# Gated cross-attention on one core: attention weights transposed in pieces of 103 rows that run across heads, whole-tile vector passes, and ScalarE exponentials of one group of heads by head

## Chip, cores and metric

One NeuronCore of a Trainium2 chip runs the whole program in one launch. The metric is the device time in microseconds, taken as the median of several executions; lower is better.

## What is computed

The reference is a decoder of four layers over `x` of 32 x 128 tokens with 128 features. Each layer adds a cross-attention step, gated by `tanh(g_xattn)`, and a feed-forward step, gated by `tanh(g_ffn)`. The change concerns the attention of layers 1, 2 and 3 (called l1x, l2x and l3x below). Cut to what matters, each of them is:

```
q = norm(x) @ Wq          # (32, 128, 128), 16 heads of 8 features
k, v = ctx @ Wk, ctx @ Wv # (32, 77, 128)
a = softmax(q_h @ k_h.T / sqrt(8))   # per head h: 128 queries x 77 keys
x = x + tanh(g_xattn[layer]) * (concat_h(a @ v_h) @ Wo + bo)
```

Layers 1 and 3 have an output bias `bo`, layer 2 has none; layer 1 has a bias on v; layer 3 adds a mask to the scores.

## The kernel before, in words

`attention` (L458) is called three times, for l1x, l2x and l3x; queries (`xnT`), keys (`kT`) and values (`vall`, 77 keys on the partitions) are already in SBUF then. It loops over 32 tiles n, one batch entry of 128 queries each. The 16 heads are four groups g of four heads i. Every engine has its program written out by hand with semaphores between them, and runs it strictly in order:

- GpSimd (`pool`): `keys(n)` (L510) spreads the keys of a tile over a 128 x 308 block, so that one group of heads becomes one matmul. `values(n)` (L517) copies the values of a tile into `Vpad`, zeroed once in `constants` (L127), with a 32-column strip per head. `divide(n)` (L522) multiplies 128 x 1232 exponentials by the reciprocal sums. `add(n)` (L533) adds the gated output to `x`; with an output bias `bias(n)` (L526) adds the gated bias too. In one step of its loop: keys(it+5), values(it+1), add(it-1), bias(it), divide(it+2).
- TensorE (`pe`): `score(n)` (L566) makes four products of 128 x 308 in PSUM banks 2 to 5 (in l3x after four mask products, L562). `turn(n, r)` (L576) transposes the weights of head r of each of the four groups (four transposes of 77 columns, into bank 6 or 7 by turns), for r = 0 to 3. `weigh(n, r)` (L586) multiplies them by the values, four narrow products side by side, summed over r. `output(n)` (L595) applies Wo. The order within a tile is turn 0, turn 1, output(n-1), weigh 0, turn 2, weigh 1, turn 3, weigh 2, score(n+4), weigh 3.
- VectorE (`v`): `shift(n)` takes the largest score of each head (L659) and subtracts it (L664) into `prob`, both in two halves of 8 heads; `total(n)` sums the exponentials in two halves (L672) and takes the reciprocal (L674); `spread` and `joined` (L680, L684) take the statistics of x for the next norm.
- ScalarE (`sc`): `keep_turned(n)` copies each transposed round out of PSUM (L634), with `keep_out(n-1)` (L625) after the second; then `exponent(n+3)` in two halves (L619), then `keep_heads(n)` (L641, L643).

TensorE's score(n+4) waits until the shift of tile n+3 has read the score banks (L559). All tiles use the same four banks, so scores are made for one tile at a time.

Of the kernel before, what the change touches and what calls it, by code (L numbers as in the profile page):

```python
# [21 lines left out]
P = 128  # L22
D = 128
# [54 lines left out]
def constants(nc, t, d):  # L78

    with ExitStack() as ctx:  # L80
# [15 lines left out]
        def _(pool):  # L96
# [29 lines left out]
            for b in range(2):  # L126
                step(pool.memset(t["Vpad"][b][:], 0.0))  # L127
# [330 lines left out]
def attention(nc, t, d, layer, gate_at, bias_v=False, bias_out=False, masked=False):  # L458
# [4 lines left out]

    AHEAD = 4
    GK = HG * KEYS
    with ExitStack() as ctx:
        s = Sems(nc, ctx, layer)
        loads, gb_ready, biased = s.one("loads"), s.one("gb_ready"), s.one("biased")
# [22 lines left out]
        def scores(i):  # L491
            return ps[:, 2 + 2 * i:4 + 2 * i, 0:GK].rearrange("p b (h k) -> p b h k", k=KEYS)

        def heads(a, i):
            return a[:, 8 * i:8 * i + 8].rearrange("p (b h) -> p b h", b=2)

        def probs(n, i):
            return prob[n % 4][:, 8 * i:8 * i + 8, :].rearrange("p (b h) k -> p b h k", b=2)

        @block.sync  # L500
        def _(sp):
            if bias_out:
                sp.dma_start(bo[:], d[f"{layer}_bo"].partition_broadcast(P)).then_inc(loads, 16)

        @block.gpsimd
        def _(pool):
# [30 lines left out]
            if bias_out:  # L537
                pool.wait_ge(loads, 16)
                pool.tensor_scalar(gb[:], bo[:], t["gate"][:, gate_at:gate_at + 1], None, ALU.mult).then_inc(gb_ready, 1)
                pool.wait_ge(gb_ready, 1)  # L540
            for it in range(1 - AHEAD, NT):
# [6 lines left out]
                if bias_out and it >= 0:  # L548
                    bias(it)
# [5 lines left out]
        def _(pe):  # L555
            def score(n):
                pe.wait_ge(kblk_ready, n + 1)
                if n >= 1:
                    pe.wait_ge(shifted, 2 * n)  # L559
# [19 lines left out]
            def weigh(n, r):  # L579
                if r == 0:  # L580
# [3 lines left out]
                pe.wait_ge(turned_kept, 4 * n + r + 1)  # L584
# [3 lines left out]
                if r == HG - 1:  # L588
                    ins.then_inc(heads_made, 1)

            def output(n):
# [23 lines left out]
        def _(sc):  # L615
            def exponent(n):
                for i in range(2):
                    sc.wait_ge(shifted, 2 * n + 1 + i)
                    sc.activation(prob[n % 4][:, 8 * i:8 * i + 8, :], prob[n % 4][:, 8 * i:8 * i + 8, :], ACT.Exp, scale=scale).then_inc(exped, 1)  # L619
# [25 lines left out]
            for n in range(AHEAD - 1):  # L645
                exponent(n)
# [2175 lines left out]
```

## Time and profile before

| | us |
|---|---|
| median of 3 runs | 1613.0 |
| range of the runs | 1606.56 to 1613.46 |
| the profiled execution | 1609.98 |
| its span in the trace | 1608.2 |
| l1x, start of the first and of the last transpose | 236.3 and 389.8 |
| l2x, the same | 770.1 and 922.9 |
| l3x, the same | 1053.8 and 1224.5 |

Over the span TensorE is busy 77%, VectorE 62%, GpSimd 55% and ScalarE 51%. These shares mix a dozen stages; the three attention stages take about 520 us of the span together, and only they are changed but for one memset. In a timeline row the first number is the start and the second the time from the start of the first of its instructions to the end of the last; the distance between the starts of successive rows of one engine is what an operation really costs that engine, since instructions overlap a little.

### The profile page before, as it was taken

The page shows a single profiled execution, that of the slowest core. Times are in us where ns is not written, and L with a number is a line of the kernel's source. Part 1 is how long each engine was busy: PE and PEld are TensorE (multiplying, and loading weights), DVE is VectorE, ACT ScalarE, POOL GpSimd, SP SyncE. Part 2 cuts the span into 40 slices and gives each one's busy share as a digit, 9 for nine tenths or more (in the row PEclk, how much of TensorE's full clock was granted, in tenths as well). Part 3 has the DMA queues.
Part 4 walks back from the last instruction along what each step waited for, and adds up shares of the span by engine and source line. Part 5 has one row for each costly group of instructions (what it writes and reads, how often), then busy time and mean ns, then how long its engine had stood idle before and what let it go on. Part 6 is the DMA issues. An engine that isn't in the chain of part 4 may idle for free. (4 is left out here: it accounts for less than half of the span.)

```text
span 1608.2 us, 27318 instructions
## 1 busy us (share of the span) xinstructions
PE 1233.3 (77%) x9890; PEld 857.0 (53%) x9890; DVE 1004.2 (62%) x2128; ACT 821.8 (51%) x1584; POOL 888.1 (55%) x1106
## 2 busy tenths in 40 slices
PE   4773569997459996444899968689997774989994
PEld 4432546664359994333566535455656553565553
DVE  5789869995531111344999769688882687443421
ACT  2487448886635453144788766467775431212120
POOL 5200148885245554651677578367775345478775
PEclk9796779999679998667899979889997795999997
DMA  2000000000238883110000000000000004344442
GB/s 102 7 0 0 1 2 2 2 2 5 59 111 240 238 230 85 40 31 9 2 1 2 2 16 1 2 2 1 2 2 1 24 33 146 76 80 97 94 88 23
DMA packets 51798, 74.98 MB, mean 47 GB/s; under 512 B 8169, under 2 KB 31602, under 8 KB 51282
## 3 DMA queue, kind: packets, MB, share of 16 engines
q1 hardware_dynamic: 35858, 55.01, 10.7%
q0 software_dynamic: 15808, 18.24, 6.8%
q8 instruction: 80, 1.31, 0.3%
q14 instruction: 52, 0.43, 0.1%
HBM read 57.09 MB, written 16.12 MB: 46 GB/s over the span
## 5 line engine op out<-in xcount | busy, mean ns | idle before, releaser
L1616 PE MATMUL ps<-topk_up_sb,topk_wu 128*128 128x512 f32 x256 | 124.1, 632 | 2.9 <-DVE sb_xnT L1736 2.2
L1517 ACT ACTIVATE topk_ga<-ps 128x512 f32<-128x512 f32 x64 | 38.3, 599 | 155.5 <-PE ps L1616 152.7
L1440 POOL DMA_INDIRECT out<-topk_shared,l3f_route_slots x64 | 100.2, 1566 | 18.1 <-issue 18.0
L1736 DVE TENSOR_TENSOR sb_xnT<-topk_ga,ps 128x512 f32<-128x512 f32 x64 | 43.9, 688 | 103.3 <-ACT topk_ga L1517 99.7
L207 POOL TENSOR_SCALAR sb_stage<-sb_x,l0f_rstd,l0f_shift 128x128 f32<-128x128 f32 x48 | 24.6, 525 | 146.3 <-DVE l0f_shift L194 146.1
L2095 DVE TENSOR_TENSOR l1f_g_y<-ps,l1f_g_wd 128x256 f32<-128x256 f32 x39 | 16.6, 425 | 136.1 <-PE ps L2038 100.2
L2065 ACT ACTIVATE l1f_g_h<-ps,l1f_g_wd 128x256 f32<-128x256 f32 x156 | 63.3, 475 | 73.6 <-DMA l1f_g_wd<-l1f_W 49.9
L522 POOL TENSOR_TENSOR l3x_prob<-l3x_prob,l3x_rden 128x1232 f32<-128x1232 f32 x32 | 72.0, 2249 | 51.1 <-DVE l3x_rden L674 51.1
L522 POOL TENSOR_TENSOR l2x_prob<-l2x_prob,l2x_rden 128x1232 f32<-128x1232 f32 x32 | 72.0, 2249 | 44.4 <-DVE l2x_rden L674 44.4
L634 ACT ACTIVATE l3x_pt<-ps 77x512 f32<-77x512 f32 x128 | 72.7, 592 | 39.7 <-PE ps L576 39.7
L522 POOL TENSOR_TENSOR l1x_prob<-l1x_prob,l1x_rden 128x1232 f32<-128x1232 f32 x32 | 72.0, 2249 | 32.5 <-DVE l1x_rden L674 32.5
L634 ACT ACTIVATE l2x_pt<-ps 77x512 f32<-77x512 f32 x128 | 72.6, 592 | 32.5 <-PE ps L576 29.1
L634 ACT ACTIVATE l1x_pt<-ps 77x512 f32<-77x512 f32 x128 | 72.7, 592 | 30.4 <-PE ps L576 29.5
L1436 POOL DMA_INDIRECT topk_xg<-l3f_rows,l3f_route_slots x64 | 76.7, 1198 | 18.9 <-issue 18.3
L1977 POOL DMA_INDIRECT l1f_g_xg<-l1f_rows,l1f_route_slots x78 | 75.2, 964 | 17.7 <-issue 12.7
L1616 PEld LDWEIGHTS ps<-topk_up_sb,topk_wu 128*128 128x128 f32 x256 | 49.7, 204 | 55.6 <-issue 50.0
L576 PE MATMUL ps<-sb_ident,l1x_prob 128*77 128x128 f32 x512 | 78.9, 288 | 0.0
L576 PE MATMUL ps<-sb_ident,l2x_prob 128*77 128x128 f32 x512 | 78.6, 287 | 0.0
L576 PE MATMUL ps<-sb_ident,l3x_prob 128*77 128x128 f32 x512 | 78.4, 286 | 0.0
L2029 PE MATMUL ps<-l1f_g_xgT,l1f_g_wu 128*128 128x256 f32 x312 | 76.0, 388 | 2.2 <-issue 2.1
L2038 PE MATMUL ps<-l1f_g_wd,l1f_g_h 128*128 128x128 f32 x624 | 75.9, 275 | 0.0
L2038 PEld LDWEIGHTS ps<-l1f_g_wd,l1f_g_h 128*128 128x128 f32 x624 | 72.7, 192 | 0.1
(500 smaller groups left out, 3588.5 us busy)
## 6 DMA issues: line engine op xcount, KB each, us to landing
l1f_g_wd<-l1f_W SPq DMA_DIRECT2D x39, 322.0 KB
l1f_g_wu<-l1f_W SPq DMA_DIRECT2D x39, 256.0 KB
topk_wu<-l3f_W SPq DMA_DIRECT2D x16, 512.0 KB
l1f_y_rows<-l1f_g_y SPq DMA_DIRECT2D x39, 128.0 KB
topk_wd<-l3f_W SPq DMA_DIRECT2D x16, 256.0 KB
l3f_rows<-l3f_route_own_rows SPq DMA_DIRECT2D x1, 2304.0 KB, 8.0
sb_x<-x SPq DMA_DIRECT2D x1, 2048.0 KB
l1f_rows<-l1f_route_own_rows SPq DMA_DIRECT2D x1, 2048.0 KB
```

Of the source, the lines that this page charges most:

```text
L522: pool.tensor_tensor(prob[n % 4][:], prob[n % 4][:], rden[n % 2][:].unsqueeze(2).broadcast_to([P, HEADS, KEYS]), ALU.mult).then_inc(normed, 1)
L576: ins = pe.transpose(ps[0:KEYS, 6 + r % 2, g * P:g * P + P], prob[n % 4][:, HG * g + r, :], t["ident"][:])
L634: sc.activation(pt[n % 2][:, r, :, :].rearrange("k h q -> k (h q)"), ps[0:KEYS, 6 + r % 2, :], ACT.Copy).then_inc(turned_kept, 1)
L1436: pool.indirect_dma_start(out=xg[g % R][:, i, :], out_offset=None, in_=u["rows"], in_offset=spot(g, i)).then_inc(row_came[g % R], 16)
L1440: pool.indirect_dma_start(out=out_rows, out_offset=spot(g, i), in_=y[g % 2][:, i, :], in_offset=None, compute_op=ALU.add).then_inc(y_added ...
L1517: sc.activation(gx[c % 2][:], ps[:, 2 * (c % 2), :], ACT.Gelu).then_inc(x_acted, 1)
L1616: ins = pe.matmul(ps[:, 2 * (c % 2) + i, :], wu[g % W][:, (i * CX + c) * P:(i * CX + c + 1) * P], xgT[g % 2][:], start=True, stop=True)
L1736: v.tensor_tensor(xh[g % 2][:, c, :], gx[c % 2][:], ps[:, 2 * (c % 2) + 1, :], ALU.mult).then_inc(x_ready, 1)
L1977: pool.indirect_dma_start(out=xg[r][:, i, :], out_offset=None, in_=u["rows"], in_offset=bass.IndirectOffsetOnAxis(ap=u["slots"][:, g * G + ...
L2029: pe.matmul(ps[:, c, 0:GS], wu[g % W][:, c * P:(c + 1) * P], xgT[g % 2][:], start=True, stop=True).then_inc(made, 1)
L2038: ins = pe.matmul(ps[:, 4 + g % 2, i * P:(i + 1) * P], h[g % 2][:, c, i * P:(i + 1) * P], wd[g % W][:, c * P:(c + 1) * P], start=(c == 0), ...
L2065: sc.activation(h[g % 2][:, c, :], ps[:, c, 0:GS], ACT.Gelu, bias=wd[g % W][:, C * P + c:C * P + c + 1]).then_inc(acted, 1)
```

## The change

Transposing goes by 103 consecutive columns of a group's 308 instead of by head: three rounds per tile (103, 103 and 102 columns) instead of four. The rows of the transposed weights then belong to more than one head, so the values have to be laid out in the same order: SyncE brings them with seven DMAs per four tiles from `vall` into `vrows`, and GpSimd multiplies them by a mask that is 1 where row and column belong to the same head. `Vpad` and its memsets go. The output bias becomes a product of one row on TensorE. VectorE takes the largest of all 16 heads in one instruction, subtracts and sums 12 heads in one instruction each; the last group's four heads are done by ScalarE alone, by head, straight from PSUM, with bias `-scale * max` (`negate`, VectorE) and the sum in the accumulator. score(n+4) now waits for this step (`direct`) too.

The core of the diff:

```diff
-            for b in range(2):
-                step(pool.memset(t["Vpad"][b][:], 0.0))
...
+    PIECES, L = 3, 103
+    FROM = [(0, 0, 0, 77), (0, 77, 0, 26), (1, 0, 26, 51), (1, 51, 0, 52), (2, 0, 52, 25), (2, 25, 0, 77), (2, 102, 0, 1)]
+    MV = 4
+    DG = GROUPS - 1
+    DH = HG * DG
...
         def _(sp):
             if bias_out:
-                sp.dma_start(bo[:], d[f"{layer}_bo"].partition_broadcast(P)).then_inc(loads, 16)
+                sp.dma_start(bo[:], d[f"{layer}_bo"].partition_broadcast(1)).then_inc(loads, 16)
+            for j in range(NT // MV):
+                if j >= 2:
+                    sp.wait_ge(vpad_ready, MV * (j - 1))
+                for c, row, key, n in FROM:
+                    sp.dma_start(vrows[j % 2][row:row + n, c, :], t["vall"][key:key + n, j * MV * P:(j + 1) * MV * P]).then_inc(v_here[j % 2], 16)
...
-                pool.tensor_copy(bass.AP(tensor=vpad[n % 2], offset=0, ap=[[HEADS * 32, KEYS], [HG * 32, GROUPS], [32 + HD, HG], [1, HD]]),
-                                 t["vall"][:, n * P:(n + 1) * P].rearrange("k (g i c) -> k g i c", g=GROUPS, i=HG)).then_inc(vpad_ready, 1)
+                j = n // MV
+                if n % MV == 0:
+                    pool.wait_ge(v_here[j % 2], 16 * len(FROM) * (j // 2 + 1))
+                pool.tensor_tensor(vpad[n % 2][:], vrows[j % 2][:, :, (n % MV) * P:(n % MV + 1) * P], vmask[:], ALU.mult).then_inc(vpad_ready, 1)
...
-            def bias(n):
-                xb = t["x"][:, n * P:(n + 1) * P]
-                pool.tensor_tensor(xb, xb, gb[:], ALU.add).then_inc(biased, 1)
...
+            step = Chain(pool, mask_step)
+            step(pool.memset(own_head[:], 1.0))
+            step(pool.affine_select(out=own_head[:], in_=own_head[:], compare_op=ALU.is_ge, fill=0.0, base=0,
+                                    pattern=[[L, PIECES], [-KEYS, HG]], channel_multiplier=1))
+            step(pool.affine_select(out=own_head[:], in_=own_head[:], compare_op=ALU.is_ge, fill=0.0, base=KEYS - 1,
+                                    pattern=[[-L, PIECES], [KEYS, HG]], channel_multiplier=-1))
+            for c in range(PIECES):
+                step(pool.tensor_copy(vmask[:, c, :].rearrange("k (g i c) -> k g i c", g=GROUPS, i=HG),
+                                      own_head[:, c, :].unsqueeze(1).unsqueeze(3).broadcast_to([L, GROUPS, HG, HD])))
...
                 if n >= 1:
-                    pe.wait_ge(shifted, 2 * n)
+                    pe.wait_ge(shifted, n)
+                    pe.wait_ge(direct, n)
...
                 for g in range(GROUPS):
-                    ins = pe.transpose(ps[0:KEYS, 6 + r % 2, g * P:g * P + P], prob[n % 4][:, HG * g + r, :], t["ident"][:])
+                    at = piece(g, c)
+                    ins = pe.transpose(ps[0:at.stop - at.start, 6 + k % 2, g * P:g * P + P], weights[:, at], t["ident"][:])
...
-                    ins = pe.matmul(ps[32 * g:32 * g + 32, 0, 0:P], vpad[n % 2][:, HG * g + r, :], pt[n % 2][:, r, g, :],
-                                    start=(r == 0), stop=(r == HG - 1), tile_position=(0, 32 * g))
+                    ins = pe.matmul(ps[32 * g:32 * g + 32, 0, 0:P], vpad[n % 2][0:rows, c, 32 * g:32 * g + 32], pt[n % 2][0:rows, c, g, :],
+                                    start=(c == 0), stop=(c == PIECES - 1), tile_position=(0, 32 * g))
...
-                pe.matmul(OUT, oT[n % 2][:], w[:, 384:512], start=True, stop=True).then_inc(out_made, 1)
+                if bias_out:
+                    pe.matmul(OUT, t["ones"][0:1, :], bo[:], start=True, stop=False)
+                pe.matmul(OUT, oT[n % 2][:], w[:, 384:512], start=not bias_out, stop=True).then_inc(out_made, 1)
...
                 weigh(n, 0)
                 turn(n, 2)
                 weigh(n, 1)
-                turn(n, 3)
-                weigh(n, 2)
                 if n + AHEAD < NT:
                     score(n + AHEAD)
-                weigh(n, 3)
+                weigh(n, 2)
...
+            def fourth(n):
+                if n >= 4:
+                    sc.wait_ge(turned, PIECES * (n - 3))
+                if n >= 2:
+                    sc.wait_ge(recip, n - 1)
+                sc.wait_ge(lower, n + 1)
+                for h in range(HG):
+                    ins = sc.activation(prob[n % 4][:, DH + h, :], scores[:, DG, h, :], ACT.Exp, bias=negmax[n % 2][:, h:h + 1], scale=scale,
+                                        accum_out=rowsum[n % 2][:, DH + h:DH + h + 1])
+                ins.then_inc(direct, 1)
+
             def exponent(n):
-                for i in range(2):
-                    sc.wait_ge(shifted, 2 * n + 1 + i)
-                    sc.activation(prob[n % 4][:, 8 * i:8 * i + 8, :], prob[n % 4][:, 8 * i:8 * i + 8, :], ACT.Exp, scale=scale).then_inc(exped, 1)
+                sc.wait_ge(shifted, n + 1)
+                sc.activation(prob[n % 4][:, 0:DH, :], prob[n % 4][:, 0:DH, :], ACT.Exp, scale=scale).then_inc(exped, 1)
...
-                for r in range(HG):
-                    if r == 2 and n >= 1:
+                for c in range(PIECES):
+                    if c == 2 and n >= 1:
                         keep_out(n - 1)
-                    sc.wait_ge(turned, 4 * n + r + 1)
-                    sc.activation(pt[n % 2][:, r, :, :].rearrange("k h q -> k (h q)"), ps[0:KEYS, 6 + r % 2, :], ACT.Copy).then_inc(turned_kept, 1)
+                    if c == 2 and n + AHEAD - 1 < NT:
+                        fourth(n + AHEAD - 1)
+                    k, rows = PIECES * n + c, min(L, GK - L * c)
+                    sc.wait_ge(turned, k + 1)
+                    sc.activation(pt[n % 2][0:rows, c, :, :].rearrange("k g q -> k (g q)"), ps[0:rows, 6 + k % 2, :], ACT.Copy).then_inc(turned_kept, 1)
...
+            def largest(n):
+                v.wait_ge(scored, n + 1)
+                v.tensor_reduce(rowmax[n % 2][:].rearrange("p (b h) -> p b h", h=HG), scores, X, ALU.max).then_inc(maxed, 1)
+
+            def negate(n):
+                v.wait_ge(maxed, n + 1)
+                if n >= 2:
+                    v.wait_ge(direct, n - 1)
+                v.tensor_scalar(negmax[n % 2][:], rowmax[n % 2][:, DH:HEADS], -scale, None, ALU.mult).then_inc(lower, 1)
+
             def shift(n):
...
+                v.tensor_tensor(prob[n % 4][:, 0:DH, :].rearrange("p (b h) k -> p b h k", h=HG), scores[:, 0:DG],
+                                rowmax[n % 2][:, 0:DH].rearrange("p (b h) -> p b h", h=HG).unsqueeze(3).broadcast_to([P, DG, HG, KEYS]),
+                                ALU.subtract).then_inc(shifted, 1)
...
             for n in range(NT):
...
+                ahead, behind = n + AHEAD - 1, n - 2
+                if ahead < NT:
+                    largest(ahead)
+                if behind >= 0:
+                    spread(behind)
+                if ahead < NT:
+                    negate(ahead)
+                    shift(ahead)
+                if ahead - 1 < NT:
+                    total(ahead - 1)
+                if behind >= 0:
+                    joined(behind)
+                if ahead - 1 < NT:
+                    invert(ahead - 1)
```

## Rows read from the trace of the kernel before

**Rows 1.** Busy time by engine, twenty tiles of l1x, then of l2x.

```profile
260.00:356.00 96.00, 92.50 (x1152) 58.93 (x1150) 95.31 (x179) 79.32 (x160) 78.74 (x99) 1.00 0.01 2
800.00:896.00 96.00, 92.50 (x1152) 58.97 (x1151) 95.31 (x178) 77.27 (x160) 70.80 (x80) 1.00 0.01 2
```

**Rows 2.** Timeline of VectorE in l1x: start, us, operation, count, idle before.

```profile
303.31 1.48 DVE L672 TENSOR_REDUCE l1x_rowsum<-l1x_prob 128x8 f32<-128x616 f32 x2
304.83 0.25 DVE L674 RECIPROCAL l1x_rden<-l1x_rowsum 128x16 f32<-128x16 f32 x1
...
305.12 1.50 DVE L659 TENSOR_REDUCE l1x_rowmax<-ps 128x8 f32<-128x616 f32 x2
306.54 1.50 DVE L664 TENSOR_TENSOR l1x_prob<-ps,l1x_rowmax 128x616 f32<-128x616 f32 x2
```

**Rows 3.** Timeline of TensorE in l1x.

```profile
304.25 0.80 PE L566 MATMUL ps<-l1x_kblk,sb_xnT 32*128 32x308 f32 x8
304.98 0.43 PE L586 MATMUL ps<-l1x_pt,sb_Vpad 77*32 77x128 f32 x8
305.33 1.10 PE L576 MATMUL ps<-sb_ident,l1x_prob 128*77 128x128 f32 x8
306.27 0.39 PE L595 MATMUL ps<-sb_wstat,l1x_oT 128*128 128x128 f32 x2
306.83 0.43 PE L586 MATMUL ps<-l1x_pt,sb_Vpad 77*32 77x128 f32 x8 [0.17 <-ACT l1x_pt L634]
307.19 0.66 PE L576 MATMUL ps<-sb_ident,l1x_prob 128*77 128x128 f32 x4
307.78 0.43 PE L586 MATMUL ps<-l1x_pt,sb_Vpad 77*32 77x128 f32 x8
```

**Rows 4.** Timeline of ScalarE in l1x.

```profile
304.49 1.31 ACT L619 ACTIVATE l1x_prob<-l1x_prob 128x616 f32<-128x616 f32 x2
305.71 0.35 ACT L641 ACTIVATE l1x_oT<-ps,sb_cols 128x128 f32<-128x128 f32 x1
306.09 1.08 ACT L634 ACTIVATE l1x_pt<-ps 77x512 f32<-77x512 f32 x2
307.07 0.36 ACT L625 ACTIVATE l1x_gated<-ps,sb_gate 128x128 f32<-128x128 f32 x1
307.89 0.59 ACT L634 ACTIVATE l1x_pt<-ps 77x512 f32<-77x512 f32 x1 [0.46 <-PE ps L576]
```

**Rows 5.** Timeline of TensorE in l3x, from one tile's mask to the next.

```profile
1101.93 0.72 PE L562 MATMUL ps<-l3x_maskall,sb_identb 128*128 128x308 bf16 x4
1102.59 0.80 PE L566 MATMUL ps<-l3x_kblk,sb_xnT 32*128 32x308 f32 x8
...
1107.42 0.70 PE L562 MATMUL ps<-l3x_maskall,sb_identb 128*128 128x308 bf16 x4
```

**Rows 6.** Timeline of ScalarE at accumulating activations of another stage.

```profile
407.65 0.27 ACT L1149 ACTIVATE ps<-ps 128x128 f32<-128x128 f32 x1
407.84 0.19 ACT L1149 ACTIVATION_READ_ACCUMULATOR ps<-ps 128x1 f32 x1
407.93 0.27 ACT L1149 ACTIVATE ps<-ps 128x128 f32<-128x128 f32 x1
```

**Rows 7.** Groups of GpSimd: the copy of the values, a product of two full tiles.

```profile
L517 POOL COPY sb_Vpad<-l2x_vall x32: 284/288/293, 768.7 to 915.9; 77x128 f32<-77x128 f32 x32
...
L1409 POOL TENSOR_TENSOR sb_xc<-topk_ga,topk_up_sb x16: 1265/1268/1274, 1262.1 to 1322.6; 128x512 f32<-128x512 f32 x16
```

**Rows 8.** Timeline of TensorE at the start of l1x: the second tile's scores.

```profile
225.94 1.41 PE L566 MATMUL ps<-l1x_kblk,sb_xnT 32*128 32x308 f32 x8 [3.13 <-DVE l1x_prob L664]
```

**Rows 9.** DMA queue of SyncE: packets, MB, share of 16 engines' span.

```profile
q1 hardware_dynamic: 35858, 55.01, 10.7%
```

**Rows 10.** Start of the kernel, GpSimd and ScalarE.

```profile
9.25 1.10 POOL L127 MEMSET sb_Vpad<- 77x512 f32 x2
...
12.01 0.21 ACT L135 ACTIVATE sb_gate<-sb_graw 128x8 f32<-128x8 f32 x1 [9.92 <-DMA sb_graw<-g_ffn]
```

More of the change, by code:

```diff
@@ L465, in attention @@
     GK = HG * KEYS
+    PIECES, L = 3, 103
[3 more added lines that the diff above has]
+    DH = HG * DG
     with ExitStack() as ctx:
         s = Sems(nc, ctx, layer)
-        loads, gb_ready, biased = s.one("loads"), s.one("gb_ready"), s.one("biased")
+        loads, mask_step, v_here = s.one("loads"), s.one("mask_step"), s.two("v_here")
         kblk_ready, scored, maxed, shifted, exped, summed, recip, normed = (
@@ L483, in attention, with piece @@
         kblk, prob = sbs("kblk", [P, GK], 2), sbs("prob", [P, HEADS, KEYS], 4)
-        pt, oT = sbs("pt", [KEYS, HG, GROUPS, P], 2), sbs("oT", [P, P], 2)
+        pt, oT = sbs("pt", [L, PIECES, GROUPS, P], 2), sbs("oT", [P, P], 2)
         rden, rowmax, rowsum = sbs("rden", [P, HEADS], 2), sbs("rowmax", [P, HEADS], 2), sbs("rowsum", [P, HEADS], 2)
-        vpad, gated = t["Vpad"], sbs("gated", [P, D], 2)
-        bo, gb = sbs("bo", [P, D], 1)[0], sbs("gb", [P, D], 1)[0]
+        vrows, vpad, gated = sbs("vrows", [L, PIECES, MV * P], 2), sbs("vpad", [L, PIECES, P], 2), sbs("gated", [P, D], 2)
+        own_head, vmask = sbs("own_head", [L, PIECES, HG], 1)[0], sbs("vmask", [L, PIECES, P], 1)[0]
+        negmax, lower, direct = sbs("negmax", [P, HG], 2), s.one("lower"), s.one("direct")
+        bo = sbs("bo", [1, D], 1)[0]
         OT, OUT = ps[:, 0, 0:P], ps[:, 1, 0:D]
         block = ctx.enter_context(nc.Block())
[L491 to L498, printed above, removed]
+        scores = ps[:, 2:6, 0:GK].rearrange("p b (h k) -> p b h k", k=KEYS)
+        def piece(g, c):
+            return slice(GK * g + L * c, GK * g + min(L * c + L, GK))
         @block.sync
@@ L547, in _ @@
                     add(it - 1)
-                if bias_out and it >= 0:
-                    bias(it)
                 if 0 <= it + AHEAD - 2 < NT:
@@ L645, in _ @@
             for n in range(AHEAD - 1):
+                fourth(n)
                 exponent(n)
@@ L655, in _, with invert @@
         def _(v):
+            def largest(n):
[6 more added lines that the diff above has]
+                v.tensor_scalar(negmax[n % 2][:], rowmax[n % 2][:, DH:HEADS], -scale, None, ALU.mult).then_inc(lower, 1)
             def shift(n):
-                v.wait_ge(scored, n + 1)
-                for i in range(2):
-                    v.tensor_reduce(heads(rowmax[n % 2], i), scores(i), X, ALU.max).then_inc(maxed, 1)
                 if n >= 4:
-                    v.wait_ge(turned, 4 * (n - 3))
-                for i in range(2):
-                    v.wait_ge(maxed, 2 * n + 1 + i)
-                    v.tensor_tensor(probs(n, i), scores(i), heads(rowmax[n % 2], i).unsqueeze(3).broadcast_to([P, 2, HG, KEYS]),
-                                    ALU.subtract).then_inc(shifted, 1)
+                    v.wait_ge(turned, PIECES * (n - 3))
+                v.wait_ge(maxed, n + 1)
+                v.tensor_tensor(prob[n % 4][:, 0:DH, :].rearrange("p (b h) k -> p b h k", h=HG), scores[:, 0:DG],
+                                rowmax[n % 2][:, 0:DH].rearrange("p (b h) -> p b h", h=HG).unsqueeze(3).broadcast_to([P, DG, HG, KEYS]),
+                                ALU.subtract).then_inc(shifted, 1)
             def total(n):
+                v.wait_ge(exped, n + 1)
+                v.tensor_reduce(rowsum[n % 2][:, 0:DH], prob[n % 4][:, 0:DH, :], X, ALU.add).then_inc(summed, 1)
+            def invert(n):
                 if n >= 2:
                     v.wait_ge(normed, n - 1)
-                for i in range(2):
-                    v.wait_ge(exped, 2 * n + 1 + i)
-                    v.tensor_reduce(rowsum[n % 2][:, 8 * i:8 * i + 8], prob[n % 4][:, 8 * i:8 * i + 8, :], X, ALU.add).then_inc(summed, 1)
-                v.wait_ge(summed, 2 * n + 2)
+                v.wait_ge(summed, n + 1)
+                v.wait_ge(direct, n + 1)
                 v.reciprocal(rden[n % 2][:], rowsum[n % 2][:]).then_inc(recip, 1)
@@ L684, in joined @@
                 v.bn_aggr(t["mv"][:, n, :], st[:, n % 2, :]).then_inc(var_ready, 1)
-            shift(0)
-            for n in range(1, AHEAD - 1):
+            for n in range(AHEAD - 1):
+                largest(n)
+                negate(n)
                 shift(n)
-                total(n - 1)
+                if n >= 1:
+                    total(n - 1)
+                    invert(n - 1)
             for n in range(NT):
-                if n + AHEAD - 1 < NT:
-                    shift(n + AHEAD - 1)
-                if n >= 2:
-                    spread(n - 2)
-                if n + AHEAD - 2 < NT:
-                    total(n + AHEAD - 2)
-                if n >= 2:
-                    joined(n - 2)
+                ahead, behind = n + AHEAD - 1, n - 2
[12 more added lines that the diff above has]
+                    invert(ahead - 1)
             for n in range(NT - 2, NT):
@@ L2675, in build @@
         sb2("stage", [P, BLK])
-        sb2("Vpad", [KEYS, HEADS, 32])
         sb2("maski", [P, 8 * KEYS], I32)
```

27 lines of the change are left out of this document (13 added, 14 removed).

## The prediction

> **What bounds the kernel now.** I read the table of busy time for twenty tiles of l1x and of l2x first [rows 1]: of 96 us VectorE is busy 95.31, TensorE 92.50, ScalarE and GpSimd under 80. Then the timelines of one tile. TensorE's rows give the period [rows 3]: 304.25 to 307.78 is 3.53, and weigh, turn, weigh (0.35, 0.59, 0.35) follow, 4.83 us a tile. VectorE fills it without a gap [rows 2]: two maxima 1.42, two subtractions 1.42, two sums 1.52, and 0.48 of small work (reciprocal and statistics). TensorE has only 0.17 of waiting. So l1x and l2x are bound by VectorE with TensorE close behind, and both must get shorter for a gain. In l3x the period is 1107.42 - 1101.93 = 5.49 [rows 5]: the mask adds 0.66 on TensorE, which is the bound there.
>
> **TensorE.** One turn (0.59) and one weigh (0.35) go per tile [rows 3]. Twelve transposes with 103 stationary columns replace sixteen with 77; the moving side stays 128 columns, so I leave their step alone and add 0.02 for the first load of a round. The bias product adds two passes; the two of the output cost 0.39 with their switch [rows 3], I take 0.2, between 0.1 and 0.4. Its own work becomes 4.66 - 0.94 + 0.04 = 3.76 (l2x), 3.96 (l1x), 4.62 (l3x).
>
> **VectorE.** Maxima stay 1232 columns, 1.35 to 1.42. Subtraction and sum fall to three quarters of 1.42 each, 1.07. `negate` adds 0.12 to 0.2; the small work stays 0.48. Sum about 4.15. The 0.1 that the reciprocal lost waiting for the second sum is now covered by `joined`.
>
> **GpSimd.** l2x shows 70.80/20 = 3.54 per tile, l1x 3.94 [rows 1]; the bias addition goes in l1x and l3x (0.40). The copy of 0.29 becomes a product of 103 x 384. Two full operands of 512 columns took 1.27 [rows 7], three quarters is 0.95; ends 0.7 and 1.27. Sum 3.54 - 0.29 + 0.95 = 4.2, at most 4.5.
>
> **ScalarE.** Three copies at 0.49 instead of four; the exponential of 924 columns in one, 1.5 x 0.61 less a start, 0.88 instead of 1.22 [rows 4]. New is the group by head. No exponential with accumulator stands in the trace; the nearest rows are squares of 128 columns with one [rows 6]: 0.19 to the start of the accumulator read, 0.09 more to the next activation, 0.28 a step. 51 columns fewer at 0.83 ns (512 columns took 0.59, 128 took 0.27 [rows 4, 6]) take off 0.04. The bias per partition adds 0.08 (the l1x copy with such a bias took 0.35 against 0.27 for 128 columns [rows 4, 6]). So 0.32 a head, and from the first start to the end of the last read 3 x 0.32 + 0.23 + 0.19 = 1.38, say 1.40. Below: if the bias costs no step, 1.06. Above: if nothing overlaps, 4 x (0.31 + 0.19) = 2.00. I take 1.40, since rows 6 are the same two instructions back to back. ScalarE's sum is 1.47 + 0.27 + 1.28 + 0.88 + 0.3 = 4.2.
>
> The Trainium skill, ScalarE: Activation LUTs, What ACT_TABLE_LOAD costs, gives about 280 ns + 0.833 ns a column for an activation with a bias by partition, less 93 ns back to back. By it the four activations would be 4 x 0.251 = 1.00 where I have 0.86, an estimate 0.14 longer a tile: some 12 us less gain, 1600. The rule speaks against cutting work into 77-column pieces; rows 6 show the same fixed cost, a little smaller.
>
> **The ring that decides.** Every engine's own sum is now at most 4.2, but score(n+4) waits for `direct` of tile n+3, which stands in ScalarE's queue behind copy 0, copy 1 and keep_out of tile n; and behind score stand weigh 2 and turn 0 of the next tile, for which copy 0 waits. Once round, from the start of copy 0: two copies 0.98, keep_out 0.27, four heads 1.40, signal to TensorE 0.15 (copy 0 ended at 306.68, weigh started at 306.83 [rows 3, 4]), score 0.73, weigh 0.35, turn to copy 0.70 (307.19 to 307.89 [rows 3, 4]) and 0.02 for the wider load: 4.60 us. Copy 2 and the exponential of 12 heads run beside score and weigh. What is queued behind the new wait is late by about 0.5 us a tile on TensorE, and that is the price. `negate` does not enter: it ends some 0.5 us before the four heads start. l3x has the mask inside the ring, 4.60 + 0.66 = 5.26.
>
> **The sum.** 28 tiles per stage make scores ahead: 4.83 to 4.60 twice and 5.49 to 5.26 save 0.23 x 84 = 19.3. The last three tiles of a stage make none and lose 0.94 of rounds each, 9 x 0.94 = 8.5, less 6 x 0.2 for the bias product, 7.3. At the start of a stage scores are made one tile after the other: one round is 3.13 + 1.41 = 4.54 at half clock [rows 8]; it becomes 1.41 + 1.43 + 0.15 + 1.40 + 0.25 of links = 4.64, nine rounds cost 0.9. At nothing I cost: GpSimd's six mask steps (some 2.5 us; the keys of the third tile then come 4 us before they are needed; without that cover 2.5 us a stage); the two memsets that go (1.10 us), since the gate waits until 12.01 for its load anyway [rows 10]; SyncE's small bias load. The execution goes from 1609.98 to 1609.98 - 19.3 - 7.3 + 0.9 = 1584.3, and the median of the runs was 3.0 above that execution: **1587**.
>
> **Values by DMA.** 309 rows of 2 KB per four tiles. Packets of that queue took 0.107 x 16 x 1608.2 / 35858 = 0.077 us [rows 9]: 1.5 us over sixteen engines, 24 us if all went through one. Four tiles last 18.4 us and the loads run four tiles ahead, so the first is hidden and the second is not. The Trainium skill, DMA: Bandwidth & Descriptors, says under How many engines (k) that the largest divisor up to 16 of the partition count sets the engines: 11, 13, 3, 13, 5, 11 and 1 here, and the first engine gets 43 rows, by that estimate 3.3 us, hidden as well. Seven issues per four tiles on SyncE have nothing beside them.
>
> **Rivals.**
> - *GpSimd becomes the bound* (0.16). If the four heads take 1.06, the ring is 4.26, next to GpSimd's 4.2. A further 0.34 x 84 = 29 us: 1558. For it: the bias cost may hide in the pipeline. Against: rows 6 show no such overlap.
> - *The four heads do not overlap at all* (0.10): 2.00, ring 5.20 in l1x and l2x, 5.86 in l3x, 0.60 x 84 = 50 us more than forecast: 1637, slower than before. It decides from about 1.71 on, where the ring's loss has eaten the whole gain of 26 us. Against it stand rows 6, for it that those rows have no bias pointer and write PSUM.
> - *Half of that* (0.16): heads at 0.39 each, 1.65 to the end, 21 us more, 1608, no difference.
> - *The change doesn't do what it says on values* (0.03): the DMAs go through one engine, 24 us per four tiles, 6.0 a tile, 1700.
>
> **Numbers.** The forecast has 0.55. The range 1558 to 1614 goes from GpSimd's bound past the half case and leaves out the two bad ones. Half a percent is 8 us, about what a measurement of this kernel tells from none: faster (under 1605) 0.76, the same 0.13, slower 0.11.
>
> **What would show it.** Right: starts of `score` 4.6 us apart in l1x and l2x and 5.26 in l3x; VectorE at some 90% with a wait for TensorE's scores before the maxima; TensorE waiting about 0.5 us a tile before score for the ScalarE line of the four heads; exponentials of 77 columns 0.32 apart. Wrong: no wait of TensorE there, GpSimd without gaps (rival one); steps of 0.5 (rival two); a wait of GpSimd for `vrows` (the last); a granted clock under 1.0 in the middle of a stage.

## The result and the profile after

| | before | after |
|---|---|---|
| median of 9 runs each, us | 1613.0 | 1598.64 |
| range of the runs | 1603.33 to 1616.44 | 1595.24 to 1606.52 |
| the profiled execution / its span | 1609.98 / 1608.2 | 1601.03 / 1599.3 |
| usual tile of l1x, l2x, l3x (start of its first transpose to the next one's; to about 0.01) | 4.83, 4.83, 5.48 | 4.81, 4.74, 5.45 |
| first to last tile of l1x, l2x, l3x | 150.36, 149.72, 167.61 | 147.58, 144.34, 165.19 |
| their sum | 467.7 | 457.1 |

The ratio is 0.993, 95% interval 0.9903 to 0.9957: faster, clear of the noise but by less than 1%. The medians are 14 us apart and the means of the runs, on which the ratio stands, 11; 26 were forecast. Of the 10.6 us that the three stages gave from their first to their last tile, 3.9 come from the 27 usual intervals of each, 2.0 from the first interval and 4.7 from the last three (4.50, 4.69 or 4.60, 4.50 became 4.48, 3.92, 3.92 in l1x and l3x and 4.40, 3.56, 3.56 in l2x). So the steady part (the first and the usual intervals, 28 a stage), which was to carry 19.3 of the 26, is what is missing: it gave 5.9. Ahead of the first transpose the stages became longer by 1.5 us in all (from the first score 14.34, 14.94 and 18.18 became 14.74, 15.35 and 18.84).

The busy table of the same stretches as [rows 1] and one of l3x, after the change (us, then PE, PEld, DVE, ACT and POOL busy, granted clock, DMA share, GB/s):

```profile
260.00:356.00 96.00, 86.42 (x960) 54.16 (x960) 84.32 (x141) 87.63 (x279) 85.78 (x81) 1.00 0.12 35
800.00:896.00 96.00, 76.52 (x932) 48.16 (x930) 94.18 (x141) 86.77 (x286) 86.49 (x82) 1.00 0.12 35
```

In l1x no engine is full any more: a ring of waits bounds it, as forecast. In l2x VectorE still shows 94.18 of 96, though its work was to fall to 4.15 a tile. That is the first thing that does not fit.

**The ring in l1x.** One tile of TensorE, against [rows 3] (start, duration, line, and in brackets the idle time before with its releaser):

```profile
367.27 1.12 PE L588 MATMUL ps<-sb_ident,l1x_prob 128*103 128x128 f32 x8
368.32 0.48 PE L609 MATMUL ps<-l1x_bo,sb_ones 1*128 1x128 f32 x2
368.74 0.49 PE L610 MATMUL ps<-sb_wstat,l1x_oT 128*128 128x128 f32 x2
369.16 0.42 PE L599 MATMUL ps<-l1x_pt,l1x_vpad 103*32 103x128 f32 x8
...
371.00 0.80 PE L575 MATMUL ps<-l1x_kblk,sb_xnT 32*128 32x308 f32 x8 [0.49 <-ACT l1x_prob L638]
371.73 0.43 PE L599 MATMUL ps<-l1x_pt,l1x_vpad 102*32 102x128 f32 x8
372.09 1.12 PE L588 MATMUL ps<-sb_ident,l1x_prob 128*103 128x128 f32 x8
```

and ScalarE beside it, against [rows 4]:

```profile
368.06 1.08 ACT L662 ACTIVATE l1x_pt<-ps 103x512 f32<-103x512 f32 x2 [0.28 <-PE ps L588]
369.26 0.37 ACT L650 ACTIVATE l1x_gated<-ps,sb_gate 128x128 f32<-128x128 f32 x1
369.53 0.32 ACT L638 ACTIVATE l1x_prob<-ps,l1x_negmax 128x77 f32<-128x77 f32 x1
369.74 0.20 ACT L638 ACTIVATION_READ_ACCUMULATOR l1x_prob<-ps,l1x_negmax 128x1 f32 x1
369.83 0.33 ACT L638 ACTIVATE l1x_prob<-ps,l1x_negmax 128x77 f32<-128x77 f32 x1
...
370.64 0.22 ACT L638 ACTIVATION_READ_ACCUMULATOR l1x_prob<-ps,l1x_negmax 128x1 f32 x1
370.73 0.62 ACT L662 ACTIVATE l1x_pt<-ps 102x512 f32<-102x512 f32 x1
...
372.87 1.08 ACT L662 ACTIVATE l1x_pt<-ps 103x512 f32<-103x512 f32 x2 [0.27 <-PE ps L588]
```

Follow it once round: copies from 368.06; `keep_out` (L650) starts 1.20 later, not 0.98, because the output it reads was begun only at 368.74 and ended at 369.23; the bias product stands ahead of it (L609, 368.32). From `keep_out` the heads start after 0.27 and end 1.33 after that, at 370.86 (370.64 + 0.22), TensorE's scores start 0.14 later, weigh 0.73 after that, turn 0.36, and the next copies 0.78 after turn starts (372.87). 1.20 + 0.27 + 1.33 + 0.14 + 0.73 + 0.36 + 0.78 = 4.81. TensorE waits 0.49 for the heads in every tile, as forecast, and the ring is the forecast one with 0.22 in a place where the forecast had none (its other terms differ by at most 0.07 and cancel).

**The negation in l2x.** VectorE, two tiles:

```profile
794.50 0.72 DVE L693 TENSOR_SCALAR l2x_negmax<-l2x_rowmax 128x4 f32<-128x4 f32 x1
795.14 1.11 DVE L699 TENSOR_TENSOR l2x_prob<-ps,l2x_rowmax 128x924 f32<-128x924 f32 x1
796.17 1.10 DVE L705 TENSOR_REDUCE l2x_rowsum<-l2x_prob 128x12 f32<-128x924 f32 x1
797.19 0.17 DVE L722 BATCH_NORM_AGGREGATE sb_mv<-l2x_st 128x2 f32<-128x6 f32 x1
797.36 0.25 DVE L712 RECIPROCAL l2x_rden<-l2x_rowsum 128x16 f32<-128x16 f32 x1
```

and GpSimd at the same time:

```profile
792.95 2.25 POOL L533 TENSOR_TENSOR l2x_prob<-l2x_prob,l2x_rden 128x1232 f32<-128x1232 f32 x1 [0.46 <-DVE l2x_rden L712]
795.16 0.70 POOL L519 TENSOR_TENSOR l2x_kblk<-l2x_kT,sb_groupmask 128x308 f32<-128x308 f32 x1
...
797.69 2.25 POOL L533 TENSOR_TENSOR l2x_prob<-l2x_prob,l2x_rden 128x1232 f32<-128x1232 f32 x1 [0.46 <-DVE l2x_rden L712]
```

`negate` works on 128 x 4 numbers and lasts 0.72 us: it ends at 795.22, GpSimd's division at 795.20. Of the 96 negations of the three stages, 91 began while a GpSimd instruction ran. 66 of these took longer than 0.175 us, and each ended 0.02 to 0.03 us after that instruction, however much of it was left (up to 0.93). The other 25 began with at most 0.15 of it left and took 0.15 to 0.17, as did the 5 that met none. The minimum, median and maximum (ns) over l2x:

```profile
L693 DVE TENSOR_SCALAR l2x_negmax<-l2x_rowmax x32: 170/724/950, 757.3 to 903.9; 128x4 f32<-128x4 f32 x32
```

It closes a second ring: from the start of the division to that of the subtraction, which follows the held negation, 2.19; then subtraction 1.03, sum 1.02, statistics 0.17 and reciprocal 0.33 to the next division at 797.69. That is 792.95 to 797.69, 4.74, the tile of l2x; its second to fifth take 4.52 to 4.64. Some 0.56 a tile of VectorE's busy time is this waiting, which explains its 94.18 (4.65 a tile; without the hold, in e2_neg_reduce below, 4.09).

### The profile page after: what moved, and what is told of

Same layout as the page of the kernel before. It is cut to its first block and busy times, and to the rows that moved or that the text cites. A ratio compares the mean times of both kernels' runs of the same rounds, so it can differ in the third digit from the quotient of the medians.

```text
span 1599.3 us, 25917 instructions
## 1 busy us (share of the span) xinstructions
PE 1182.9 (74%) x8865; PEld 821.5 (51%) x8866; DVE 962.7 (60%) x1936; ACT 855.7 (54%) x2160; POOL 934.2 (58%) x1056
## 5 line engine op out<-in xcount | busy, mean ns | idle before, releaser
L687 DVE TENSOR_REDUCE l3x_rowmax<-ps 128x16 f32<-128x1232 f32 x32 | 46.1, 1442 | 43.3 <-PE ps L575 43.3
L2198 POOL DMA_INDIRECT l2x_c_yg<-l1f_y_rows,sb_dest x64 | 61.2, 956 | 14.7 <-issue 13.6
L2076 PEld LDWEIGHTS ps<-l1f_g_xgT,l1f_g_wu 128*128 128x128 f32 x312 | 57.3, 194 | 11.6 <-issue 4.7
L662 ACT ACTIVATE l3x_pt<-ps 103x512 f32<-103x512 f32 (+1 forms) x96 | 54.5, 601 | 16.0 <-PE ps L588 16.0
L687 DVE TENSOR_REDUCE l1x_rowmax<-ps 128x16 f32<-128x1232 f32 x32 | 46.1, 1442 | 27.9 <-PE ps L575 27.9
L662 ACT ACTIVATE l2x_pt<-ps 103x512 f32<-103x512 f32 (+1 forms) x96 | 54.4, 600 | 14.8 <-PE ps L588 14.8
```

Source lines behind the costliest of these rows:

```text
L662: sc.activation(pt[n % 2][0:rows, c, :, :].rearrange("k g q -> k (g q)"), ps[0:rows, 6 + k % 2, :], ACT.Copy).then_inc(turned_kept, 1)
L687: v.tensor_reduce(rowmax[n % 2][:].rearrange("p (b h) -> p b h", h=HG), scores, X, ALU.max).then_inc(maxed, 1)
L2076: pe.matmul(ps[:, c, 0:GS], wu[g % W][:, c * P:(c + 1) * P], xgT[g % 2][:], start=True, stop=True).then_inc(made, 1)
L2198: pool.indirect_dma_start(out=yg[n % R][:, c, :], out_offset=None, in_=t["y_rows"], in_offset=bass.IndirectOffsetOnAxis(ap=t["dest"][:, c ...
```

## The experiments

Ratios are against the kernel before on the same chip in the same session; chips differ by 2%, so only ratios are compared between sessions, and tile lengths, which agree between sessions. Tile lengths are read to about 0.01. In the first session (e1 to e4) the ratios give more than the stages do, for e3_both 36 us against 27.5; there is no profile of the kernel before from that session, so where the rest lies is not shown, and the argument goes by tiles and stages.

| run | ratio [95%] | l1x | l2x | l3x | sum of the stages |
|---|---|---|---|---|---|
| before | 1 | 4.83 | 4.83 | 5.48 | 467.7 |
| the change | 0.993 [0.9903, 0.9957] | 4.81 | 4.74 | 5.45 | 457.1 |
| e5_changed_again | 0.9914 [0.989, 0.9937] | 4.81 | 4.74 | 5.44 | 457.0 |
| e1_bias_early | 0.9817 [0.9789, 0.9845] | 4.74 | 4.74 | 5.21 | 447.3 |
| e2_neg_reduce | 0.9896 [0.9864, 0.9928] | 4.81 | 4.58 | 5.45 | 457.8 |
| e3_both | 0.9772 [0.9751, 0.9793] | 4.58 | 4.58 | 5.20 | 440.2 |
| e4_whole | 0.9733 [0.9709, 0.9756] | 4.54 | 4.54 | 4.89 | 427.5 |
| e6_heads_first | 0.9782 [0.9752, 0.9812] | 4.69 | 4.32 | 5.54 | 445.9 |
| e7_pieces | 0.9791 [0.976, 0.9822] | 4.72 | 4.72 | 4.89 | 437.0 |
| e8_passes | 0.9989 [0.9967, 1.0012] | 4.83 | 4.83 | 5.49 | 471.5 |
| e9_whole_pool | 0.965 [0.9604, 0.9696] | 4.54 | 4.54 | 4.63 | 419.5 |
| e10_best | 0.9641 [0.9606, 0.9677] | 4.54 | 4.32 | 4.62 | 414.7 |
| e11_loads_once | 0.9923 [0.9891, 0.9956] | 4.81 | 4.74 | 5.44 | 457.0 |

The changed kernel was run once more in the second session (e5_changed_again), so that its neighbours there have it beside them:

> The changed kernel once more, beside the others of this set: a ratio to the kernel before of 0.990 to 0.996 as measured, periods of 4.81, 4.74 and 5.45 us again, and the negation at 0.72 us in most tiles of l2x.

It came out as the first time, tile by tile.

### Is the bias product in the ring? (e1_bias_early)

```diff
             def output(n):
...
-                if bias_out:
-                    pe.matmul(OUT, t["ones"][0:1, :], bo[:], start=True, stop=False)
                 pe.matmul(OUT, oT[n % 2][:], w[:, 384:512], start=not bias_out, stop=True).then_inc(out_made, 1)
+
+            def begin(n):
+                if bias_out:
+                    if n >= 1:
+                        pe.wait_ge(out_kept, n)
+                    pe.matmul(OUT, t["ones"][0:1, :], bo[:], start=True, stop=False)
...
                 weigh(n, 1)
+                begin(n)
                 if n + AHEAD < NT:
                     score(n + AHEAD)
```

> The product of the output bias is issued after weigh 1, in TensorE's idle time before score, instead of in front of the output product. Theory A (in l1x and l3x keep_out waits for bias and output product, so the ring runs through them): keep_out starts at 0.98 after copy 0 instead of 1.21, the period of l3x goes from 5.45 to about 5.23, that of l1x from 4.81 to 4.6, or to the 4.74 of l2x if the hold of the negation (theory B) is next; l2x stays. In all 8 to 12 us less than the changed kernel. Rival R (the wider pieces or the DMAs of the values slow every tile): periods stay within 0.02.

The bias product now stands where TensorE waits for the heads anyway. l1x fell from 4.81 to 4.74 and l3x from 5.45 to 5.21; l2x, which has no bias, stayed. In l1x `keep_out` again starts 0.96 after the copies, but the heads start 0.43 after it instead of 0.27. ScalarE:

```profile
340.87 1.08 ACT L667 ACTIVATE l1x_pt<-ps 103x512 f32<-103x512 f32 x2 [0.28 <-PE ps L588]
341.83 0.37 ACT L655 ACTIVATE l1x_gated<-ps,sb_gate 128x128 f32<-128x128 f32 x1
342.26 0.33 ACT L643 ACTIVATE l1x_prob<-ps,l1x_negmax 128x77 f32<-128x77 f32 x1
```

and VectorE's negation, held until 342.15:

```profile
341.42 0.73 DVE L698 TENSOR_SCALAR l1x_negmax<-l1x_rowmax 128x4 f32<-128x4 f32 x1
```

So the first ring was shortened, and l1x came to stand in the second one, at the 4.74 of l2x.

### Is the negation's length the hold? (e2_neg_reduce)

```diff
+            step(pool.tensor_scalar(t["groupmask"][96:128, :], t["groupmask"][96:128, :], float(HD) ** -0.5, None, ALU.mult))
...
-                    ins = sc.activation(prob[n % 4][:, DH + h, :], scores[:, DG, h, :], ACT.Exp, bias=negmax[n % 2][:, h:h + 1], scale=scale,
+                    ins = sc.activation(prob[n % 4][:, DH + h, :], scores[:, DG, h, :], ACT.Exp, bias=negmax[n % 2][:, h:h + 1],
...
-                v.tensor_scalar(negmax[n % 2][:], rowmax[n % 2][:, DH:HEADS], -scale, None, ALU.mult).then_inc(lower, 1)
+                v.tensor_reduce(negmax[n % 2][:], rowmax[n % 2][:, DH:HEADS].unsqueeze(2), X, ALU.max, negate=True).then_inc(lower, 1)
```

> The negation of the largest scores is a tensor_reduce with negate over a length of one instead of a tensor_scalar; the scale 8^-0.5 that it applied is put into the mask of the last head group once, at the start. Theory B (VectorE's tensor_scalar from SBUF to SBUF is held until GpSimd's running instruction ends): the negation takes 0.1 to 0.2 us in every tile, where it took 0.72 in most tiles of l2x, and l2x goes from 4.74 to about 4.58 a tile; l1x and l3x stay, where the bias is the limit. In all some 4 us less. Rival C (the negation is late for another reason, its wait for the maximum or for the heads before): it keeps its 0.72.

The same values of the same size go in and out, by another instruction. VectorE's group in l2x:

```profile
L694 DVE TENSOR_REDUCE l2x_negmax<-l2x_rowmax 128x4 f32<-128x4 f32 x16 | 2.2, 140 | 0.0
```

0.14 in nearly every tile of the three stages and never over 0.16, whatever GpSimd does, and l2x falls from 4.74 to 4.58. l1x and l3x keep their length, since the other ring holds them. The sum of the stages hides the gain: the last two intervals of l3x are long (6.2 and 6.4 us instead of 3.9), and there the granted clock, 1.00 in the 5 us before (TensorE busy 4.69 of them), is 0.59 and then 0.50, the lower of its two levels:

```profile
1170.00:1176.00 6.00, 5.43 (x36) 3.78 (x40) 2.40 (x8) 3.18 (x8) 4.44 (x4) 0.59 0.00 0
1176.00:1184.00 8.00, 7.79 (x58) 4.67 (x55) 0.48 (x2) 3.23 (x7) 2.82 (x3) 0.50 0.00 0
```

That cost what l2x gave; why the clock fell in this run there is open.

### Both (e3_both)

> Both edits. Theories A and B together: 4.6 us a tile in l1x, 4.58 in l2x, 5.23 in l3x, 0.21, 0.16 and 0.22 less over 28 tiles each, 16 us less than the changed kernel, about 1583 and close to what the prediction gave. If ScalarE (busy 87.6 of 96 us in l1x) is the real bound, under 5 us come.

4.58, 4.58 and 5.20. The forecast ring was 4.60, 4.60 and 5.26. With the two omitted terms taken out, the prediction's ring is right to 0.06 us a tile. The stages together are 27.5 us shorter than before, where 25.7 were forecast, but that is partly luck: the last three intervals gave 5.4 instead of 7.3, and the first ones 1.4 that were not counted. TensorE still waits for the heads:

```profile
305.62 0.80 PE L576 MATMUL ps<-l1x_kblk,sb_xnT 32*128 32x308 f32 x8 [0.20 <-ACT l1x_prob L644]
```

### What the heads on ScalarE are worth (e4_whole, e7_pieces, e8_passes)

e4_whole keeps everything of the change but the heads: VectorE subtracts and sums all 16, ScalarE takes one exponential of 1232 columns, `fourth`, `negate` and the semaphore `direct` go.

```diff
-    DG = GROUPS - 1
+    DG = GROUPS
...
                     pe.wait_ge(shifted, n)
-                    pe.wait_ge(direct, n)
```

> Only half of the change: pieces of 103 and one pass per tile over all 16 heads; no group by head on ScalarE, no negation, and score waits for the subtraction alone. VectorE then does 1.35 + 0.20 + 1.35 + 1.37 + 0.29 = 4.56 a tile, TensorE 4.0 in l1x, 3.8 in l2x, 4.8 in l3x. Theory D (the ring through the heads costs more than the shorter passes of VectorE bring): 4.56 to 4.6 in l1x and l2x, 4.85 to 4.95 in l3x, some 20 to 26 us less than the changed kernel. Rival (relief of VectorE is what the change lives on): l1x and l2x at 4.8 or above, as before the change, and only l3x gains.

The shortest so far, 12.7 us of stages less than e3_both, most of it in l3x. Its l1x shows why:

```profile
260.00:356.00 96.00, 91.17 (x1017) 57.07 (x1016) 95.45 (x128) 74.60 (x128) 90.45 (x85) 1.00 0.12 35
```

VectorE is full at 4.54 a tile. TensorE has one wait before its scores, and it is put down to the keys:

```profile
343.64 0.80 PE L574 MATMUL ps<-l1x_kblk,sb_xnT 32*128 32x308 f32 x8 [0.21 <-POOL l1x_kblk L519]
```

e7_pieces goes one step further back and gives VectorE its six half passes again (two maxima, two subtractions, two sums), with everything else as in e4_whole:

> Only the pieces of 103, with the values by DMA and mask and the bias product: VectorE works in two halves on all 16 heads as before, no heads on ScalarE. VectorE's sum is that of before less the 0.1 of the reciprocal's wait, so l1x and l2x go from 4.83 only to about 4.75, and l3x, which TensorE bounds, from 5.48 to about 4.95: 15 to 20 us less than before. If the pieces help nothing, l3x stays at 5.4.

l1x and l2x take 4.72, 0.18 more than with whole passes, and VectorE is full again (in l1x 95.36 of 96). l3x, which TensorE bounds, stays at 4.89. e8_passes is the kernel before with whole passes alone:

```diff
-                for i in range(2):
-                    v.wait_ge(exped, 2 * n + 1 + i)
-                    v.tensor_reduce(rowsum[n % 2][:, 8 * i:8 * i + 8], prob[n % 4][:, 8 * i:8 * i + 8, :], X, ALU.add).then_inc(summed, 1)
+                v.wait_ge(exped, n + 1)
+                v.tensor_reduce(rowsum[n % 2][:], prob[n % 4][:], X, ALU.add).then_inc(summed, 1)
```

> Only the whole passes: the kernel before with one maximum, one subtraction, one exponential and one sum over all 16 heads a tile, four turns of 77. VectorE's sum falls to 4.56 but TensorE's own is 4.66 plus 0.17 of waiting: l1x and l2x at 4.75 to 4.83, l3x at 5.48 as before; 0 to 6 us less than before. That half and the pieces would each give little alone where VectorE and TensorE stand side by side.

VectorE's busy time in l2x falls from 95.31 to 91.58 of 96 [rows 1], and no usual tile gets shorter (two at the start of l2x are long, 7.7 and 6.2 us, at a granted clock of 0.50 and 0.71). The busy table:

```profile
800.00:896.00 96.00, 92.60 (x1157) 58.89 (x1158) 91.58 (x120) 75.42 (x139) 70.48 (x81) 1.00 0.01 2
```

and the one wait of a tile on TensorE, as in [rows 3]:

```profile
343.87 0.43 PE L586 MATMUL ps<-l1x_pt,sb_Vpad 77*32 77x128 f32 x8 [0.17 <-ACT l1x_pt L633]
```

VectorE now waits 0.22 a tile for the scores, where it had no gap before. So TensorE's own queue with the 0.17 it waits for the first copy, 4.66 + 0.17 = 4.83, is enough to hold the kernel before, and relieving the engine with the largest busy share alone brings nothing. VectorE stood right beside it, though: with TensorE relieved instead (e7_pieces) its six half passes still take 4.72. The pieces of 103 relieve TensorE (0.9791 alone), the whole passes are worth nothing before that and 0.18 a tile behind it (0.9733 together), and the heads on ScalarE, put where they are, take back most of it (0.991 to 0.993).

### Heads ahead of keep_out (e6_heads_first)

On top of e3_both, `fourth` moves ahead of `keep_out` in ScalarE's queue.

> On top of the bias product moved and the negation as a reduction: ScalarE does the four heads before keep_out, so that keep_out leaves the ring. If the ring from copy 0 over copy 1, the four heads, score, weigh 2 and the next turn decides, its 4.58 in l2x loses the 0.27 of keep_out: 4.3 to 4.4 in l1x and l2x, where ScalarE's and GpSimd's own sums of 4.2 come close, and 4.95 in l3x; some 15 to 20 us less than with both edits alone. Rival: GpSimd's addition waits for the later keep_out and holds up the division; then the period stays at 4.58.

Right in l2x (4.32) and wrong in the stages with a bias. TensorE in l1x:

```profile
302.69 0.37 PE L615 MATMUL ps<-l1x_bo,sb_ones 1*128 1x128 f32 x1 [0.52 <-ACT l1x_gated L656]
```

The bias product issued early needs the output bank free, which `keep_out` does, and that now stands behind the heads; `score` stands behind the bias product. The early bias product was good with the heads behind `keep_out` (e1, e3), and the heads first are good where there is no bias product (l2x); together they make a third ring. The wait shows it; no run has the heads first without the early bias product in a stage with a bias.

### A version that beats both (e9_whole_pool, e10_best)

e9_whole_pool is e4_whole with l3x's bias added by GpSimd again.

> The kernel with pieces and whole passes in every stage (the run e4_whole), with the bias of l3x alone added by GpSimd again, as in the kernel before. In e4_whole a tile of l3x took 4.89 us and one of l1x and l2x 4.54. If l3x is bound there by TensorE's own instructions, of which the bias product and the slower turn pair beside it take 0.41 us and some 0.1, a tile of l3x falls to 4.5 to 4.7; GpSimd's own sum there rises to about 4.65 (4.24 and an addition of 0.41), which would then be the bound. l1x and l2x stay at 4.54. Together 4 to 6 us less than e4_whole, a ratio to the kernel before of about 0.970. If the ring of waits and not TensorE bounds l3x, its tile stays at 4.89 or gets longer.

l3x falls from 4.89 to 4.63. TensorE's turn pair and output, without the bias product (L602, L624) and with it (L587, L608, L609) in e4_whole:

```profile
1100.36 1.12 PE L602 MATMUL ps<-sb_ident,l3x_prob 128*103 128x128 f32 x8
1101.32 0.39 PE L624 MATMUL ps<-l3x_w,l3x_oT 128*128 128x128 f32 x2
1101.89 0.42 PE L613 MATMUL ps<-l3x_pt,l3x_vpad 103*32 103x128 f32 x8 [0.18 <-ACT l3x_pt L663]
```

```profile
1071.31 1.12 PE L587 MATMUL ps<-sb_ident,l3x_prob 128*103 128x128 f32 x8
1072.36 0.48 PE L608 MATMUL ps<-l3x_bo,sb_ones 1*128 1x128 f32 x2
1072.78 0.49 PE L609 MATMUL ps<-l3x_w,l3x_oT 128*128 128x128 f32 x2
1073.19 0.43 PE L598 MATMUL ps<-l3x_pt,l3x_vpad 103*32 103x128 f32 x8
```

From turn to weigh 1.53 against 1.88, so the bias product costs TensorE 0.35 a tile net: 0.42 of its own and 0.11 in the rows beside it (turn pair 1.05 against 0.96, output 0.41 against 0.39), less the 0.18 that TensorE waits for the copy without it. GpSimd is now the bound of l3x, as expected: 100.00 of 100 us busy, at 4.63 a tile. VectorE, full at 4.54 in l1x, stands right behind it with 99.58.

```profile
1060.00:1160.00 100.00, 95.08 (x1079) 57.69 (x1082) 99.58 (x129) 72.23 (x131) 100.00 (x108) 1.00 0.11 33
```

e10_best takes for each stage its own best: whole passes with the bias product in l1x, heads first with the reduction in l2x, e9's l3x.

> The best of each stage put together: l1x with whole passes and the bias by TensorE (4.54 us a tile), l2x with the heads on ScalarE ahead of the gate's mask and the negation by a reduction (4.32 measured in e6_heads_first), l3x with whole passes and the bias by GpSimd (4.7 or below). If the stages don't act on each other the sum of the tiles is about 139 + 132 + 144 = 415 us, some 12 us less than e4_whole: ratio to the kernel before 0.965 to 0.967. The rival, that a stage's drain and the next one's start give it back: no lower than e9_whole_pool.

The tiles are as expected, 4.54, 4.32 and 4.62, and the stages sum to 414.7, 53 less than before. The ratio is 0.9641; e9_whole_pool, simpler and with no heads on ScalarE at all, has 0.965, and the 4.8 us between their stages are smaller than the intervals of the whole. In l2x GpSimd bounds e10_best (79.25 of 80 us busy):

```profile
800.00:880.00 80.00, 70.17 (x858) 44.55 (x854) 75.56 (x130) 75.52 (x256) 79.25 (x74) 1.00 0.11 34
```

### The loads of the values (e11_loads_once)

Later tiles use the values of the first eight, so three quarters of the strided loads are left out.

```diff
-            for j in range(NT // MV):
-                if j >= 2:
-                    sp.wait_ge(vpad_ready, MV * (j - 1))
+            for j in range(2):
...
-                if n % MV == 0:
-                    pool.wait_ge(v_here[j % 2], 16 * len(FROM) * (j // 2 + 1))
+                if n % MV == 0 and j < 2:
+                    pool.wait_ge(v_here[j % 2], 16 * len(FROM))
```

> The changed kernel with its strided value loads issued for the first eight tiles of each stage alone; later tiles compute with those values, so 3 of 4 of these transfers are left out. If the value loads are hidden, as the prediction said, the tiles stay at 4.81, 4.74 and 5.45 us and the time within 0.3% of the changed kernel. If they hold TensorE or GpSimd up (the rival on the loads), the tiles get shorter, by 0.05 us or more.

Nothing moves (4.81, 4.74, 5.44; sum 457.0 against 457.1): the loads are hidden.

## Why the prediction was wrong

The direction and the kind of limit came as forecast; the size did not (26 us forecast, 14 by the medians and 11 by the ratio), and two steps of the ring are to blame.

- **The direction and the kind of limit: right.** Every engine got slack in l1x and l3x, TensorE waits for the heads (0.49 a tile, forecast about 0.5), and the ring from copies over heads, scores and turn sets the tile.
- **The ring's term "keep_out 0.27 right behind two copies 0.98": this step failed.** It took `keep_out(n-1)` as following on ScalarE's queue alone. It also waits for the output product, and the change puts the bias product ahead of that. Before, the output was made in the shadow of the copies [rows 3, 4]; now it ends 1.17 after the first copy starts. I had costed the bias product on TensorE's sum only, where there was slack, and not as a releaser. 1.20 instead of 0.98, and 0.06 more from turn to copy (0.78 against 0.72): 4.81 instead of 4.60. e1_bias_early takes it out, and l3x drops by 0.24.
- **"`negate` does not enter: it ends some 0.5 us before the four heads start": failed.** I gave it 0.12 to 0.2, from its size. It lasts until GpSimd's running instruction ends, up to 0.95 us, eats the 0.5 (in l2x the heads start 0.12 after its end, at 795.34), and delays the subtraction, sum and reciprocal, on which the next division waits. This is the whole of l2x's loss (4.74 against 4.58 in e2_neg_reduce), and e1 and e3 together show it in l1x. The Trainium skill has the rule that I should have weighed: SBUF — State Buffer, under Terms, says that VectorE and GpSimd share a pair of ports by an exclusive lock held for the full instruction. The rows agree that the wait ends with the other engine's instruction, and show that it depends on the instruction's form: a scalar multiplication of 128 x 4 was held, a reduction of the same 128 x 4 never. That it is this lock which holds it, no run here shows.
- **The bias product "0.2, between 0.1 and 0.4": mis-sized.** 0.42 from its start to the output's start, some 0.53 with what it adds beside it, 0.35 net of the wait it fills (e9 against e4). TensorE's own work in l1x is therefore 4.33 (86.42 us at 4.81 a tile), not 3.96, and in l3x 4.87 (79.67 of 80 us at 4.89 in e4_whole), not 4.62. The bias product is a term of the last three tiles too, where a stage with a bias came to 3.92 and not to 3.76, and so part of why these gave 4.7 instead of 7.3; the other part is that the first of the three still waits.
- **The heads "0.32 each, 1.40 to the end": right.** 0.30 a head, 1.33 to the end. The end "nothing overlaps, 2.00" fell. The estimate by the Trainium skill (ScalarE: Activation LUTs), 0.14 longer a tile, fell as well; its 1600 meets the measured time, but by a term that isn't there.
- **VectorE 4.15, GpSimd 4.2, ScalarE 4.2 and TensorE's 3.76 in l2x: right in size.** VectorE has 4.09 without the hold and TensorE 3.79 (e2_neg_reduce, l2x); ScalarE has 4.2 in l2x and 4.4 in l1x. GpSimd has 86.49 us for 20.25 tiles, 4.27, and the product of the values measured 1.00 (forecast 0.95). The maximum 1.44, the subtraction and the sum 1.11 and 1.10 with an overlap of 0.08 each.
- **"l1x and l2x are bound by VectorE with TensorE close behind": TensorE's queue alone holds 4.83,** by e8_passes, and VectorE is no more than close to it; it did not enter the sum. Both did have to get shorter.
- **The start of a stage "nine rounds cost 0.9": under-sized.** It lost 1.5 in all ahead of the first transposes (3.23 against 3.13 of wait at the second tile's scores in l1x); the first intervals gained 2.0 in all, which I had not counted.
- **Hidden parts** (value loads, mask steps, memsets): nothing shows against them. e11 confirms the loads, and e4_whole, which has the mask steps too, reaches its first transpose in l1x and l2x as soon after its first score as the kernel before (14.34 and 14.94).
- **The rivals.** "Half of that" (1608) is 9 us from the measured median, about as far as the forecast (1587, 12 us), and its mechanism is wrong: it put the loss into longer heads.

## What to carry to other kernels

A ring of waits is summed from each step's last releaser, so for every instruction in it ask what else it waits for, and whether the change puts new work ahead of that; work costed at nothing on an engine with slack can still stand ahead of a releaser. Before cutting the engine with the highest busy share, see whether another engine's queue with its small waits already gives the period. And a small VectorE instruction beside long GpSimd ones deserves a look at its minimum, median and maximum, not at its size.

## What the hardware showed that I had not expected

A VectorE scalar multiplication of 128 x 4 fp32 numbers from SBUF to SBUF took 0.15 to 0.17 us alone and up to 0.95 when a GpSimd instruction was running, ending 0.02 to 0.03 us after it in each of the 66 cases that took over 0.175; the same data through a reduction with negation took 0.14 to 0.16 in all 96 cases. Four exponentials of 77 columns from PSUM with a bias by partition and a sum ran 0.30 us apart, each starting 0.09 after the start of the accumulator read before it (the reads lasted 0.19 to 0.24). A one-row product of 128 columns delayed the product behind it by 0.42 us (368.32 to 368.74), as much as the full 128 x 128 product behind it cost (368.74 to 369.16).
